# Self-attention over 64 latents: keys normed first, the queries' norm moved onto the scores, scores and probabilities kept dense

## What is computed

```python
xn = _layernorm(x, ln_g, ln_b)
q = split_heads(xn @ Wq.T); k = split_heads(xn @ Wk.T); v = split_heads(xn @ Wv.T)
q = _rmsnorm(q, q_gamma) * SCALE
k = _rmsnorm(k, k_gamma)
sim = jnp.einsum('bhid,bhjd->bhij', q, k)
attn = jax.nn.softmax(sim, axis=-1)
out = jnp.einsum('bhij,bhjd->bhid', attn, v)
return out.transpose(0, 2, 1, 3).reshape(b, n, DIM) @ Wo.T + bo
```

## Time and profile before

| what | value |
|---|---|
| three runs, us | 495.06, 496.59, 496.73 (median 496.59) |
| the profiled execution, us | 494.71 |
| its span, first to last instruction, us | 492.9 |
| what lies around the span, us | 1.8 |
| PE busy share of the span | 95% |
| mean granted clock of PE | 0.990 |

### The profile page before, as it was taken

One profiled execution on the slowest core, in us unless ns is written; L12 is line 12 of the kernel. 1 busy time (PEld: TensorE's weight loads), 2 busy tenths in 40 slices (PEclk: granted clock), 3 DMA queues, 4 the chain that ended last, 5 costly groups with the idle time before them and its releaser, 6 DMA issues.

```text
span 492.9 us, 8751 instructions
## 1 busy us (share of the span) xinstructions
PE 467.9 (95%) x3642; PEld 399.5 (81%) x3642; DVE 267.8 (54%) x459; ACT 238.4 (48%) x419; POOL 109.7 (22%) x101
## 2 busy tenths in 40 slices
PE   8998999999999999999988999998999899889997
PEld 7887989898988899999765659984666798778697
DVE  2657131444255232320465989947577466469897
ACT  2576333355254241521135867814788262237772
POOL 1121000010000000000201848964000000019695
PEclk9999999999999999999999999996999999999999
DMA  8925300025000200000496999950000093164000
GB/s 286 404 96 160 162 0 1 1 75 182 1 1 0 86 1 1 1 1 1 162 424 257 300 348 418 410 246 1 2 1 1 3 396 127 76 255 173 0 1 12
DMA packets 13079, 62.53 MB, mean 127 GB/s; under 512 B 1295, under 2 KB 3727, under 8 KB 7280
## 3 DMA queue, kind: packets, MB, share of 16 engines
q1 hardware_dynamic: 11024, 54.27, 29.0%
q0 software_dynamic: 2016, 7.70, 4.4%
HBM read 61.84 MB, written 0.13 MB: 126 GB/s over the span
## 4 chain that ended last, share of the span: by engine, by line
PE 79%; DVE 8%; ACT 5%; POOL 3%; issue 3%; DMA 1%; SPq 0%; DVEq 0%; ACTq 0%; POOLq 0%
PE W L1406 19%; PE W L1362 15%; PE W L1553 9%; PE W L1600 7%; PE W L1640 4%; PE W L1673 4%; PE W L1379 3%; PE W L1285 2%; PE W L1690 2%; POOL w_lo L534 2%; PE W L1428 2%; POOL small L542 1%; PE W L1623 1%; PE W L1545 1%; PE W L1469 1%
## 5 line engine op out<-in xcount | busy, mean ns | idle before, releaser
L1406 PE MATMUL W<-probs_turned_hi,ctx_split_hi 128*128 128x256 f32 x256 | 72.8, 285 | 2.5 <-issue 2.5
L1406 PE MATMUL W<-probs_turned_hi,ctx_split_lo 128*128 128x256 f32 x256 | 72.4, 283 | 0.0
L1406 PE MATMUL W<-probs_turned_lo,ctx_split_hi 128*128 128x256 f32 x256 | 72.4, 283 | 0.0
L542 POOL TENSOR_TENSOR small<-small,const 128x1 f32<-128x1 f32 (+2 forms) x9 | 6.6, 730 | 241.9 <-DVE small L989 122.1
L918 DVE TENSOR_TENSOR probs_turned_lo<-W,probs_turned_hi 128x512 fp32r<-128x512 f32 x32 | 20.6, 686 | 65.2 <-ACT probs_turned_hi L645 65.2
L1406 PEld LDWEIGHTS W<-probs_turned_hi,ctx_split_hi 128*128 128x128 f32 x256 | 49.1, 192 | 3.7 <-issue 3.3
L1600 PE MATMUL W<-w_hi,acts 128*128 128x256 f32 x272 | 49.9, 285 | 1.0 <-DVE acts L890 1.0
L534 POOL TENSOR_TENSOR w_lo<-arena,w_hi 128x320 fp32r<-128x320 f32 x32 | 42.1, 1331 | 34.1 <-ACT w_hi L587 33.9
L883 DVE TENSOR_TENSOR w_lo<-arena,w_hi 128x704 fp32r<-128x704 f32 (+1 forms) x36 | 46.1, 1319 | 6.3 <-ACT w_hi L587 5.8
L1406 PEld LDWEIGHTS W<-probs_turned_lo,ctx_split_hi 128*128 128x128 f32 x256 | 49.1, 192 | 0.2
L1406 PEld LDWEIGHTS W<-probs_turned_hi,ctx_split_lo 128*128 128x128 f32 x256 | 49.1, 192 | 0.0
(11 more groups left out here) (354 smaller groups left out, 871.5 us busy)
## 6 DMA issues: line engine op xcount, KB each, us to landing
arena<-units_dram SPq DMA_DIRECT2D x22, 1024.0 KB, 9.5
ctxmem<-units_dram SPq DMA_DIRECT2D x16, 1024.0 KB, 11.7
fixed<-units_dram SPq DMA_DIRECT2D x6, 1024.0 KB, 6.0
pbuf<-ctx_dram POOLq DMA_DIRECT2D x4, 512.0 KB, 6.4
ctxmem<-ctxT_dram SPq DMA_DIRECT2D x8, 256.0 KB, 11.5
ctxmem<-ctx_dram SPq DMA_DIRECT2D x2, 1024.0 KB, 14.6
scr<-ctx_dram POOLq DMA_DIRECT2D x3, 512.0 KB, 4.4
vecs<-vectors_dram POOLq DMA_DIRECT2D x1, 1040.0 KB, 7.7
```

What stands on the lines that cost most here:

```text
L1406: mm = pe.matmul(ps, CXN[a][:, t, c * P:(c + 1) * P], PT[z][:, t, :], start=(t == 0 and n == 0), stop=(t == KEYT - 1 and n == 2))
```

## The change

- The product for keys comes first, then queries, then values, 256 columns each, and the values a second time with the two batches' rows swapped (`VSW`), so that values of either batch lie on either half of the partitions.
- Keys are squared, normed and multiplied by both gammas (multiplied together once, early in the cross-attention) while the queries are only copied (`QR`). The queries are transposed and copied unnormed. Their norm is made after the keys' and multiplied onto the scores.
- The scores are made by 8 products of 64 by 64, one for each head and batch, dense in two PSUM banks; the four pick-out copies go. DVE takes the maximum from PSUM with two instructions, and four instructions subtract it and multiply by the queries' norm.
- The probabilities are one dense 256-wide tile; two transposes and one copy of 256 take the place of four and one of 512. The product with the values is again 8 products of 64 by 64.
- `stay_warm(6, 14)` goes, `stay_warm(4, 17)` becomes 12. POOL's zeroing goes; POOL raises 4 numbers a row twice in place of 8 once.
- The weight halves of `f1e0` are prepared later: the first behind the exponential (ACT) and the probabilities (DVE), the second behind the output copy and the norm.
- In the gate, the small product stands between the two halves of `f1b`, the three copies to `gtok` behind the first expert's scaling, and `f1b` is released after its second half, as before.

```diff
@@ -538,7 +539,8 @@
                 pool.wait_ge(ev("var_ready"), n + 1)
-                src, dst, wide = {RSQRT_QK: (ssq, rqk, 8), RSQRT_PAIR: (ve2, rstd2, 2)}.get(n, (ve, rstd, 1))
+                src, dst, wide = {RSQRT_K: (ssq[:, 0:HA], rqk[:, 0:HA], HA), RSQRT_Q: (ssq[:, HA:], rqk[:, HA:], HA),
+                                  RSQRT_PAIR: (ve2, rstd2, 2)}.get(n, (ve, rstd, 1))
                 pool.tensor_tensor(dst, src, c_("neghalf").to_broadcast([P, wide]), ALU.pow)\
...
@@ -549,13 +551,10 @@
                             pool.dma_start(gatew, gate_in).then_inc(ev("gatew_in"), 16)
-                if n == 1:
-
-                    pool.memset(PA, 0.0).then_inc(ev("pa_zero"), 1)
-                if n == 4:
+                if n == 5:
                     for p in range(SLOTS, MOE0):
                         keep_w(1, p)
-                if n == 5:
+                if n == 6:
...
@@ -692,18 +691,25 @@
             keep_xT(bank(1))
-            act.wait_ge(ev("qkv_ps"), 1)
-            act.activation(SQ, bank(2), ACT.Square).then_inc(*tick("sq_ready"))
-            act.wait_ge(ev("qkv_ps"), 2)
-            act.copy(vsb[:, :], bank(3)[:, 0:DIM]).then_inc(ev("v_sb"), 1)
-            act.wait_ge(*made("qkT_ps"))
-            act.copy(QKT, bank(4).rearrange("p (t m) -> p t m", t=4)).then_inc(*tick("qkT_sb"))
-            keep_w_hi("f1e0")
+            act.wait_ge(*made("kA_ps"))
+            act.activation(SQ[:, 0], bank(2)[:, 0:DIM], ACT.Square).then_inc(*tick("sqk_ready"))
+            act.wait_ge(*made("qA_ps"))
+            act.copy(QR, bank(3)[:, 0:DIM]).then_inc(*tick("qr_sb"))
+            act.activation(SQ[:, 1], bank(3)[:, 0:DIM], ACT.Square).then_inc(*tick("sqq_ready"))
+            act.wait_ge(*made("vA_ps"))
+            act.copy(vsb[:, :], bank(6)[:, 0:DIM])
+            act.copy(VSW, bank(7)[:, 0:DIM]).then_inc(ev("v_sb"), 1)
+            act.wait_ge(*made("qTA_ps"))
+            act.copy(QKT[:, 0:2], bank(4)[:, 0:DIM].rearrange("p (t m) -> p t m", t=2)).then_inc(*tick("qTA_sb"))
+            act.wait_ge(*made("kTA_ps"))
+            act.copy(QKT[:, 2:4], bank(5)[:, 0:DIM].rearrange("p (t m) -> p t m", t=2)).then_inc(*tick("kTA_sb"))
             act.wait_ge(*made("simA_max"))
             act.activation(SA, SA, ACT.Exp, scale=DH0 ** -0.5).then_inc(*tick("simA_exp"))
+            keep_w_hi("f1e0", [0])
             act.wait_ge(*made("ptA_ps"))
-            act.copy(PTA, bank(7).rearrange("p (t m) -> p t m", t=4)).then_inc(*tick("ptA_sb"))
+            act.copy(PTA, bank(5)[:, 0:DIM].rearrange("p (t m) -> p t m", t=2)).then_inc(*tick("ptA_sb"))
             keep_xT(bank(0))
+            keep_w_hi("f1e0", [1])
...
@@ -969,6 +975,8 @@
                     dve.tensor_tensor(NVL, bc(v_("nv"), 1, 2), bc(c_("headof"), 2, DH0), ALU.mult).then_inc(*tick("nv_ready"))
+                    gammas = v_("qk_gamma")
+                    step(dve.tensor_tensor(gammas[:, 0:DH0], gammas[:, 0:DH0], gammas[:, DH0:], ALU.mult))
                     step(dve.tensor_tensor(x[:, :], x[:, :], v_("ln_bias"), ALU.add))
...
@@ -998,38 +1006,37 @@
             step(dve.tensor_tensor(x[:, :], x[:, :], v_("bo"), ALU.add))
-            dve.wait_ge(*made("sq_ready"))
-            step(dve.tensor_reduce(ssq, SQ.rearrange("p (h d) -> p h d", h=8), AX_X, ALU.add))
-            qk4 = QK.rearrange("p (n h d) -> p n h d", n=2, h=HA)
-            rsqrt(dve.tensor_scalar(ssq, ssq, 1.0 / DH0, 1e-16, ALU.mult, ALU.max),
-                  lambda: dve.tensor_tensor(qk4, bank(2).rearrange("p (n h d) -> p n h d", n=2, h=HA),
-                                            bc(v_("qk_gamma").rearrange("p (n d) -> p n d", n=2), 2, HA), ALU.mult))
-            qk8 = QK.rearrange("p (h d) -> p h d", h=8)
-            dve.tensor_tensor(qk8, qk8, bc(rqk, 2, DH0), ALU.mult).then_inc(*tick("qk_ready"))
+            dve.wait_ge(*made("sqk_ready"))
+            step(dve.tensor_reduce(ssq[:, 0:HA], SQ[:, 0].rearrange("p (h d) -> p h d", h=HA), AX_X, ALU.add))
+            kn4 = KN.rearrange("p (h d) -> p h d", h=HA)
+            rsqrt(dve.tensor_scalar(ssq[:, 0:HA], ssq[:, 0:HA], 1.0 / DH0, 1e-16, ALU.mult, ALU.max),
+                  lambda: dve.tensor_tensor(kn4, bank(2)[:, 0:DIM].rearrange("p (h d) -> p h d", h=HA),
+                                            bc(v_("qk_gamma")[:, 0:DH0], 1, HA), ALU.mult))
+            dve.tensor_tensor(kn4, kn4, bc(rqk[:, 0:HA], 2, DH0), ALU.mult).then_inc(*tick("kn_ready"))
+            dve.wait_ge(*made("sqq_ready"))
+            step(dve.tensor_reduce(ssq[:, HA:], SQ[:, 1].rearrange("p (h d) -> p h d", h=HA), AX_X, ALU.add))
+            rsqrt(dve.tensor_scalar(ssq[:, HA:], ssq[:, HA:], 1.0 / DH0, 1e-16, ALU.mult, ALU.max))
             dve.wait_ge(*made("simA_ps"))
-            sa4 = SA.rearrange("p (i m) q -> p i m q", m=2)
-            for b in range(B):
-                for m in range(2):
-                    ins = dve.tensor_copy(sa4[b * NQ:(b + 1) * NQ, :, m, :],
-                                          bank(5 + m)[b * NQ:(b + 1) * NQ, 0:2 * TOK]
-                                          .rearrange("p (i t) -> p i t", i=2)[:, :, b * NQ:(b + 1) * NQ])
+            for m in range(2):
+                ins = dve.tensor_reduce(smax[:, 2 * m:2 * m + 2], bank(m)[:, 0:2 * NQ].rearrange("p (i q) -> p i q", i=2),
+                                        AX_X, ALU.max)
             step(ins)
-            step(dve.tensor_reduce(smax, SA, AX_X, ALU.max))
-            dve.tensor_tensor(SA, SA, bc(smax, 2, NQ), ALU.subtract).then_inc(*tick("simA_max"))
+            for h in range(HA):
+                i, m = h // 2, h % 2
+                ins = dve.tensor_scalar(SA[:, h], bank(m)[:, i * NQ:(i + 1) * NQ], smax[:, 2 * m + i:2 * m + i + 1],
+                                        rqk[:, HA + h:HA + h + 1], ALU.subtract, ALU.mult)
+            ins.then_inc(*tick("simA_max"))
             dve.wait_ge(*made("simA_exp"))
             step(dve.tensor_reduce(ssum, SA, AX_X, ALU.add))
             step(dve.reciprocal(srec, ssum))
-            dve.wait_ge(ev("pa_zero"), 1)
-            for b in range(B):
-                lo, hi = b * NQ, (b + 1) * NQ
-                ins = dve.tensor_tensor(PA[lo:hi, :, lo:hi], SA[lo:hi], bc(srec[lo:hi], 2, NQ), ALU.mult)
-            ins.then_inc(*tick("probsA"))
-            keep_w_lo("f1e0")
+            dve.tensor_tensor(PA, SA, bc(srec, 2, NQ), ALU.mult).then_inc(*tick("probsA"))
+            keep_w_lo("f1e0", [0])
             dve.wait_ge(*made("outA_ps"))
             step(dve.tensor_tensor(x[:, :], bank(2)[:, 0:DIM], x[:, :], ALU.add))
             give(norm(x[:, :], hn[:, :], 1e-5))
+            keep_w_lo("f1e0", [1])
             keep_w_lo("f1e1", [0])
...
@@ -1043,9 +1050,6 @@
             dve.wait_ge(ev("gmix_ready"), 1)
-            dve.tensor_copy(gtok[0:NQ, 0:E], gmix[0:NQ, 0, :]).then_inc(ev("gtok_ready"), 1)
-            dve.tensor_copy(gtok[NQ:P, 0:E], gmix[NQ:P, 1, :]).then_inc(ev("gtok_ready"), 1)
-            dve.tensor_copy(gtok[:, E:E + 1], c_("ones")[:, 0:1]).then_inc(ev("gtok_ready"), 1)
             for e in range(E):
...
@@ -1053,6 +1057,10 @@
                                              op0=ALU.mult, op1=ALU.subtract).then_inc(ev("xl_ready"), 1)
+                if e == 0:
+                    dve.tensor_copy(gtok[0:NQ, 0:E], gmix[0:NQ, 0, :]).then_inc(ev("gtok_ready"), 1)
+                    dve.tensor_copy(gtok[NQ:P, 0:E], gmix[NQ:P, 1, :]).then_inc(ev("gtok_ready"), 1)
+                    dve.tensor_copy(gtok[:, E:E + 1], c_("ones")[:, 0:1]).then_inc(ev("gtok_ready"), 1)
                 if e >= 2:
...
@@ -1486,33 +1494,51 @@
             wo = unit("att")[:, KT * 768:].rearrange("p (k n) -> p k n", k=KT)
-            for lo, hi in ((0, 512), (512, 768)):
+            for done, bk, lo in (("kA_ps", 2, DIM), ("qA_ps", 3, 0)):
                 for k in range(KT):
-                    mm = pe.matmul(W[1][:, lo:hi], xT[:, k, :], wa[:, k, lo:hi], start=(k == 0), stop=(k == KT - 1))
-                mm.then_inc(ev("qkv_ps"), 1)
-            stay_warm(6, 14)
-            pe.wait_ge(*made("qk_ready"))
-            for t in range(4):
-                mm = pe.transpose(bank(4)[:, t * P:(t + 1) * P], QK[:, t * P:(t + 1) * P], ident)
-            mm.then_inc(*tick("qkT_ps"))
-            pe.wait_ge(*made("qkT_sb"))
+                    mm = pe.matmul(bank(bk)[:, 0:DIM], xT[:, k, :], wa[:, k, lo:lo + DIM], start=(k == 0), stop=(k == KT - 1))
+                mm.then_inc(*tick(done))
+            for k in range(KT):
+                pe.matmul(bank(6)[:, 0:DIM], xT[:, k, :], wa[:, k, 2 * DIM:], start=(k == 0), stop=(k == KT - 1))
+            for k in range(KT):
+                for b in range(B):
+                    mm = pe.matmul(bank(7)[(1 - b) * NQ:(2 - b) * NQ, 0:DIM], xT[:, k, b * NQ:(b + 1) * NQ], wa[:, k, 2 * DIM:],
+                                   start=(k == 0), stop=(k == KT - 1))
+            mm.then_inc(*tick("vA_ps"))
+            pe.wait_ge(*made("qr_sb"))
```

(42 more changed lines are left out.)

15 lines of the change are left out of this document (8 added, 7 removed).

## The result

The changed kernel takes 493.21 us (median of five runs, 492.28 to 494.12) where the kernel before takes 496.59: a ratio of 0.9947, 95% interval [0.9928, 0.9966]. The prediction was 492.1 us, range 489.4 to 494.8. The profiled execution after took 493.21 us, its span is 491.2 and its mean granted clock 0.986 (before: 494.71, 492.9 and 0.990).

A forecast was written before the change was run, and what follows sets the result against it. Self-attention was taken as bound by one dependent chain of short operations across engines. Gains 2.0 + 0.6 + 0.4 + 0.45 - 0.05 = 3.4, plus 1.05, say 4.5 us, off 496.59 gave 492.1 us, range 489.4 to 494.8.

The forecast's parts named there:

- the same distance from there to the end: Sign expected in the profile after: time from the experts' first layer to the end of the span unchanged.
- Until the scores can be reduced: Self-attention from the keys' product to the row maximum: 2.0 us gained, with the queries' norm the later one.
- The low end of the range: 489.4 us: powers of 0.88 and short returns give 5.6 us gained, and the low-clock stretch another 1.6.
- Softmax and probabilities: Self-attention: 0.6 us gained by taking the maximum from PSUM without copies, 0.4 by one dense probabilities operation.
- To the output: From transposes to `wo`: fewer transposes and a narrower copy gain 0.45 us; the value product takes 0.05 more.
- The gate: Small product between the base halves: `gmix` starts 0.9 us earlier and `gtok` copies mostly fill idle time; 1.05 us gained.
- Rival (b): The gate gives nothing because its second base half ends later than thought: 3.4 us gained, 493.2 us; chance 0.07.
- Weight halves and transfers: Moved `f1e0` weight preparation costs 0 under cover; transfers behind `f1b` keep 2.8 us of cover.
- Rival (a): Self-attention's 64 by 64 products run one after another: 1.85 us gained, 494.7 us; chance 0.09.
- The sum: Total gain: 3.4 us up to `wo` plus 1.05 at the gate, 4.45, say 4.5 us.
- Rival (c): Clock falls in self-attention with the fill gone: 496.5 us, no change, up to 503 us, slower; chance 0.08.
- a width of 1.6 us: Range allowance for the later cross-attention's low-clock stretch being a third longer or shorter, of 4.6 us cost.

The follow-up runs named there:

- norms_together: The changed kernel with both norms made together in one POOL power of 8 a row, ahead of the transposes; 494.84 us, ratio 0.999.
- values_late_only: The changed kernel with only the swapped values' product and its copy moved behind the scores; ran once, 491.15 us.
- sums_early_only: The changed kernel with only the queries' sums and their power moved ahead of the keys' multiply; ran once, 493.59 us.
- gate_back: The changed kernel with the gate's old order: both base halves ahead of the small product, `gtok` copies right behind `gmix`; 491.07 us, ratio 0.9909.
- fill_later: The changed kernel plus nine identity products in PE's idle wait near the start of the later cross-attention; 487.34 us, ratio 0.9843.
- before_with_fill: The kernel before, without the change, plus the nine identity products of fill_later in the later cross-attention; 492.31 us, ratio 0.9914.
- late_with_fill: The changed kernel with the edits of values_late and fill_later together; 488.04 us, ratio 0.9821.
- values_late: The changed kernel with swapped values behind the scores and the queries' sums and power ahead of the keys' multiply; 491.68 us, ratio 0.9902.
- norm_in_exp: The changed kernel with the queries' norm applied as the scale of four ACT exponentials, DVE subtracting the maximum in two instructions; 492.19 us, ratio 0.9912.

## Why the prediction was right

The time lies in the range, and the mechanism is the one forecast: a chain shortened by 4.88 us where 4.45 were forecast. That the median came out only 1.1 us from the forecast is in part luck: two steps were off in opposite directions (0.8 too little, 0.3 too much), and the clock behind the first layer, which the sum took as unchanged, took back 1.7 us in the profile, more than the 0.4 gained beyond the sum. Of the signs named, "the same distance from there to the end" failed (228.05 for 226.35), and the queries' norm did not come last. By its steps:

- **Until the scores can be reduced**, 2.0 predicted, 2.80 measured (the maximum starts 5.85 us behind the first matmul, before 8.65). The step that was off is the queries' norm, set to come last at 6.7 us. It came at 5.6: its power ended at 5.53. A return from POOL took 0.11 us where I took 0.46, two powers 1.02 each for 1.14. The 0.46 was the issue piece of one power in the earlier trace rows, which in the changed kernel has no like; norms_together, with a power of 8 as before, also shows 0.11 (247.97 to 248.08), so the width is not the reason, and the reason stays open. So the scores were the later ones, by 0.2 to 0.3 us, as values_late_only and sums_early_only show. The low end of the range has the same flaw: its 5.6 us gained let the norm come 1.2 earlier, while the prediction's own scores end at 246.6 at best, which leaves 0.7 of that.
- **Softmax and probabilities**, 0.6 + 0.4 predicted. From the start of the maximum to that of the transposes are 3.26 us, before 3.97: 0.71. The probabilities' 0.4 was right. Mis-sized are the four small operations with two per-row scalars: I had 1.3 us for the maximum and these, of which the maximum took its 0.5, and they took 1.10 where 0.8 were left; with one such scalar they take 0.86 (norms_together), so most of the miss is the second scalar. This gain and the next are read from the rows; no run takes the dense scores or the dense probabilities back alone.
- **To the output**, 0.45 - 0.05 predicted, 0.37 measured (2.09 us from the transposes to `wo` for 2.46).
- **The gate**, 1.05 predicted, 1.00 measured, and undone by gate_back to 0.01 us. Rival (b) falls. As the prediction had it, DVE's weight part, and no longer the small product, is what `gmix` (L1049, 261.77) now follows; the small product was done 0.55 us earlier, at 261.22:

```profile
260.60 0.62 PE L1597 MATMUL W<-pbuf,const 128*128 128x16 f32 x4
260.63 1.23 DVE L889 TENSOR_TENSOR w_lo<-arena,w_hi 128x1024 fp32r<-128x1024 f32 x1
```

- **Weight halves and transfers**, cost 0: that weight part starts 7.29 us behind `wo`'s first matmul (260.63 - 253.34), before 7.28, so the moved halves delay nothing; and fill_later and before_with_fill have the same rest (222.35 and 222.31). Nothing of the change is paid for behind the first layer but through the clock. The 0.55 us between the small product and `gmix` are still to be had; no run tries it.
- **Rival (a)** falls: the 16 score instructions took 0.50 us and the 16 of the value product 0.74, on average 0.016 and 0.034 us from start to start. Its premise is half wrong: the scores use all four quarters of the array, but in the value product each row half writes its own half of the partitions, so only two quarters are used. The Trainium skill, TensorEngine Tiling (Array Packing), Restrictions and Gotchas, says that different row tiles can't use one PSUM bank at once; the value product, whose row halves write one bank, does not show that price, 1.4 us in the prediction. Whether the shared bank or the two quarters make it slower than the scores was not tried.
- **The sum**, 4.45 predicted, 4.88 measured, 4.9 to 5.0 with the low stretch out of both kernels. (The top of the range, 496.59 - 3.3 + 1.6, is 494.9 and not 494.8; nothing hangs on it.)
- **The clock.** Rival (c) did not occur in the changed kernel's two profiles as it was put, in the self-attention (where norms_together and values_late_only show it can). But the low stretch behind it took part of the gain, which I had only as a width of 1.6 us. Over the profiles, the rest goes with the time at 0.50 in it:

| low clock in the rest, us | rest, us |
|---|---|
| 0 | 222.35 (fill_later), 222.31 (before_with_fill) |
| 3.41 | 223.32 (late_with_fill) |
| 10.24 | 226.35, 226.11 (before), 226.14 (gate_back), 225.85 (norms_together), 225.80 (values_late_only) |
| 13.65 | 228.05, 227.80 (changed), 228.10 (values_late) |
| 17.07 | 228.68 (norm_in_exp), 228.51 (sums_early_only) |

So 10.24 us cost 3.5 to 4.0 (I had 4.6 from the earlier trace rows), and over all rows a microsecond at 0.50 costs 0.3 to 0.4. The kernel before and the changed one stand on one line: what the change did to the rest is to come upon 13.65 us in place of 10.24 in both of its profiles.

This clock and the openings account for the two profiled executions (4.88 - 1.5 - 1.7 = 1.7 us, which is the difference of their spans). That they are also why the median fell by 3.4 and not 4.9 is argued, since the other runs were not profiled. The opening is no matter of the change: before_with_fill, which has the opening of the kernel before, also began late (242.76). Why the low stretch is longer behind the changed self-attention stays open. gate_back has 10.24 us in its profile and a mean clock of 0.990 in five of six runs, so the order at the gate may bear on it, or only the moment at which the later wait falls; no run here sets the moment alone.

## What to carry to other kernels

A chain of short dependent operations is shortened by what is split off it: taking the keys' half of the norm first and the queries' half beside the transposes was worth 2.3 of 4.9 us. Compare stages by offsets from a common instruction before medians: 1 us of a stage is plain there and lost in a total where the clock moves by more. And before tuning a stage, look at the clock's line: one fill of nine products in an idle wait gave the kernel before 4.0 us (496.28 to 492.31), nearly what this change is worth.

## What was not expected of the hardware

- A DVE operation of 64 numbers a row from PSUM costs 0.27 us with two per-row scalars and 0.22 with one, one of 128 without them 0.25 (1.10 / 4, 0.86 / 4, 0.49 / 2).
- A POOL power of 4 a row costs 1.02 us, so with the earlier trace rows 0.88, 1.02 and 1.65 for 2, 4 and 8; two asked for together took 2.35 us.
- A stretch at 1.2 GHz cost 0.3 to 0.4 us per us here, where an estimate from half speed alone would be 0.5. Why it is less was not looked into.
- The clock fell also behind rows in which PE shows almost no gap: 3.50 of 3.50 us (late_with_fill), 3.38 and 3.39 of 3.40 us (norm_in_exp, sums_early_only).
